# Last group's value product from 32x32 tiles without the DRAM trip, two output tiles ahead of it, last stores on two queues

## The chip, the core and the metric

One core of a Trainium2 chip runs the kernel. The metric is device time in microseconds for one execution; the kernel before takes 1820.34 us (median of 3 runs, 1820.07 to 1821.33). TensorE multiplies, VectorE (DVE) and ScalarE (ACT) work on SBUF and PSUM, GpSimd (POOL) on SBUF, SyncE (SP) mainly issues DMAs.

## What is computed

A cross attention over 32 batches of 512 tokens, 640 channels, 20 heads of 32, with 77 context tokens a batch, then an output projection with bias and the residual. All in fp32. (The reference has three more attention branches; the context has only 77 tokens, so their slices are empty and they add nothing.)

```python
q = _heads(hidden_states @ to_q_w)
h_txt = _sdpa(q, _heads(ehs_txt @ to_k_w), _heads(ehs_txt @ to_v_w))
...
s = jnp.einsum('bhqd,bhkd->bhqk', q, k) * scale      # in _sdpa
p = jax.nn.softmax(s, axis=-1)
return jnp.einsum('bhqk,bhkd->bhqd', p, v)
...
out = _merge(h_txt) + ...
out = out @ to_out_w + to_out_b
out = (out + residual) / RESCALE
```

## The kernel before

It has two stages. `project_context` (about the first 300 us) computes keys and values of all batches and leaves them in DRAM (`k_scratch`, `v_scratch`). `attend` goes over 32 batches, and in each over 5 groups of 4 heads (128 channels). Group n = 5 b + g, 0 to 159. Most matmuls of the projections are three passes over operands split into a high and a low part (`project_q` L750, `project_out` L789: 5 channel chunks x 3 passes = 15 matmuls of 512 columns for one tile).

A group's steps: `scores` (L765, 16 matmuls, each on 32 rows of the array, into four PSUM banks `s_bank`, one for a head), `maxima` (DVE L638), `exps` (ACT L597), `reciprocals` (DVE L644), `normalise` (POOL L574), `turn_probs` (DVE L654: 32x32 squares of the probabilities are transposed into `turned`). The squares are not yet a matrix with the 77 context tokens on the partitions: SyncE writes `turned` to DRAM (`write_probs`, L522, 768 KB) and reads it back in three pieces (`read_probs`, L530) into `probs_t`, which has tokens on 77 partitions and 512 queries along the free dimension. In `turned` partition i*32+s holds context token s of a 32-token block, for the queries of row block i. `sum_values` (L777) multiplies values and probabilities, 4 matmuls, one for a head, each 77 rows by 32 columns by 512 moving. Its result is copied by `ot_high_part` (ACT L604) and the remainder by `ot_low_part` (DVE L665) into `o_t`. `project_out` of tile k (L789) reads `o_t` of all five groups of a batch; `add_output` (DVE L685) adds bias and residual, `turn_output` (DVE L692) turns the tile into `out_blocks`, and `store_out` (SP L518) sends it out in four DMAs once all five tiles are turned. There is one `out_blocks`, so `turn_output` of a batch waits until the stores of the batch before have landed.

The order on each engine is written by hand in strings, one for each group of a batch. In the one of TensorE, S is the scores, Q the query projection of the next group, V the value product of the group two back, O and P an output tile of the batch before or the one before that:

```python
TENSOR = orders("S Q0 Q1 Q2 Q3 Q4 P3 V",
                "S Q0 Q1 Q2 Q3 Q4 P4 V",
                "S Q0 Q1 Q2 Q3 Q4 O0 V",
                "S Q0 Q1 Q2 Q3 Q4 O1 V",
                "S O2 Q0 Q1 Q2 Q3 Q4 V")
```

What the last batch leaves open stands behind the loop: the value products of groups 158 and 159, tiles 3 and 4 of batch 30, and the five tiles of batch 31. `project_out` writes two PSUM banks in turn, so tile n waits until tile n - 2 has been added (`out_added`).

## Time and profile before

| | us |
|---|---|
| median of 3 runs | 1820.34 |
| lowest, highest | 1820.07, 1821.33 |
| the profiled run | 1821.04 |
| its span, first to last instruction | 1819.2 |

The profile is one execution. PE is TensorE's matmuls, PEld its weight loads, which overlap them. Times in its rows count from the start of the span. A row of a timeline merges instructions of one kind: start, time that it covers, engine, line, operation, what it writes and reads, how many (an fp32 matmul leaves two records, so four are x8), and in brackets how long the engine had been idle and what ended that. "SPq" rows are DMA issues on SyncE.

### The profile page before, as it was taken

The page shows a single profiled execution, that of the slowest core. Times are in us where ns is not written, and L with a number is a line of the kernel's source. Part 1 is how long each engine was busy: PE and PEld are TensorE (multiplying, and loading weights), DVE is VectorE, ACT ScalarE, POOL GpSimd, SP SyncE. Part 2 cuts the span into 40 slices and gives each one's busy share as a digit, 9 for nine tenths or more (in the row PEclk, how much of TensorE's full clock was granted, in tenths as well). Part 3 has the DMA queues.
Part 4 walks back from the last instruction along what each step waited for, and adds up shares of the span by engine and source line. Part 5 has one row for each costly group of instructions (what it writes and reads, how often), then busy time and mean ns, then how long its engine had stood idle before and what let it go on. Part 6 is the DMA issues. An engine that isn't in the chain of part 4 may idle for free.

```text
span 1819.2 us, 38127 instructions
## 1 busy us (share of the span) xinstructions
PE 1756.4 (97%) x13360; PEld 1364.8 (75%) x13360; DVE 1282.9 (71%) x2506; ACT 1052.6 (58%) x5597; POOL 496.5 (27%) x735
## 2 busy tenths in 40 slices
PE   7999996799999999999999999999999999999996
PEld 7999995567777777777777777777777777777764
DVE  5321201678888888888888888888888888888873
ACT  4321211666666666666666666666666666666660
POOL 1111110333333333333333333333333333333330
PEclk9999998899999999999999999999999999999998
DMA  9543112587888888888888888888888888888863
GB/s 229 152 121 92 63 47 58 142 204 214 224 220 223 222 222 224 226 219 221 225 227 219 223 223 223 230 215 222 223 224 229 217 224 223 223 224 224 220 185 103
DMA packets 311599, 357.00 MB, mean 196 GB/s; under 512 B 40240, under 2 KB 194592, under 8 KB 311408
## 3 DMA queue, kind: packets, MB, share of 16 engines
q1 hardware_dynamic: 241648, 301.30, 61.0%
q10 hardware_dynamic: 65472, 40.64, 10.4%
q0 software_dynamic: 4288, 12.62, 2.0%
q8 instruction: 106, 1.74, 0.4%
q14 instruction: 85, 0.70, 0.1%
HBM read 174.10 MB, written 180.39 MB: 195 GB/s over the span
## 4 chain that ended last, share of the span: by engine, by line
PE 78%; DVE 2%; ACT 1%; DMA 1%; issue 1%; POOL 0%; SPq 0%; ACTq 0%; DVEq 0%
PE p_bank L750 31%; PE p_bank L789 29%; PE p_scores L765 9%; PE p_bank L777 8%; ACT probs L597 1%; DVE negmax L638 0%; DMA p_scratch<-turned 0%; DMA out<-out_blocks 0%; DVE turned L654 0%; POOL probs L574 0%; DMA probs_t<-p_scratch 0%; DVE x_t L676 0%; DVE x_raw L671 0%; DVE out_blocks L692 0%; SPq L518 0%
## 5 line engine op out<-in xcount | busy, mean ns | idle before, releaser
L597 ACT ACTIVATE probs<-p_scores,negmax 128x77 f32<-128x77 f32 x2560 | 788.7, 361 | 325.9 <-DVE negmax L638 325.9
L574 POOL TENSOR_TENSOR probs<-probs,rsum 128x308 f32<-128x308 f32 x640 | 447.4, 701 | 1021.1 <-DVE rsum L644 1021.0
L597 ACT ACTIVATION_READ_ACCUMULATOR probs<-p_scores,negmax 128x1 f32 x2560 | 619.5, 242 | 0.0
L750 PE MATMUL p_bank<-x_t,wq_split 128*128 128x512 f32 x2400 | 596.4, 401 | 16.0 <-DVE x_t L676 16.0
L789 PE MATMUL p_bank<-o_t,wo_split 128*128 128x512 f32 x2400 | 574.9, 391 | 0.4 <-DVE x_turned L685 0.4
L750 PEld LDWEIGHTS p_bank<-x_t,wq_split 128*128 128x128 f32 x2400 | 446.8, 190 | 116.3 <-DVE x_t L676 17.2
L789 PEld LDWEIGHTS p_bank<-o_t,wo_split 128*128 128x128 f32 x2400 | 448.7, 188 | 98.0 <-issue 2.5
L654 DVE STREAM_TRANSPOSE turned<-probs 128x384 f32<-128x384 f32 x640 | 352.4, 551 | 39.9 <-POOL probs L574 39.8
L765 PEld LDWEIGHTS p_scores<-k_sb,q_t 32*128 32x128 f32 x5120 | 159.8, 187 | 152.8 <-issue 152.8
L638 DVE TENSOR_REDUCE negmax<-p_scores 128x16 f32<-128x1232 f32 x160 | 230.2, 1438 | 24.0 <-PE p_scores L765 23.8
L604 ACT ACTIVATE o_t<-p_bank 128x512 fp32r<-128x512 f32 x160 | 98.5, 616 | 177.3 <-PE p_bank L777 177.3
L765 PE MATMUL p_scores<-k_sb,q_t 32*128 32x77 f32 x5120 | 182.5, 279 | 18.6 <-ACT probs L597 11.6
L644 DVE RECIPROCAL rsum<-sums 128x4 f32<-128x4 f32 x640 | 107.5, 168 | 125.7 <-ACT probs L597 121.2
L777 PE MATMUL p_bank<-probs_t,v_sb 77*32 77x512 f32 x1280 | 171.3, 607 | 8.6 <-DMA probs_t<-p_scratch 6.3
L661 DVE COPY q_t<-p_bank 128x512 f32<-128x512 f32 x160 | 109.4, 684 | 81.4 <-PE p_bank L750 81.4
L377 PE MATMUL p_bank<-ctx_t,wk_split 128*128 128x256 f32 (+1 forms) x1200 | 147.2, 285 | 9.9 <-DVE wk_split L315 9.6
L377 PEld LDWEIGHTS p_bank<-ctx_t,wk_split 128*128 128x128 f32 x1200 | 146.2, 195 | 10.2 <-DVE wk_split L315 9.6
L397 PE MATMUL p_bank<-wv_split,ctx_t 128*128 128x320 f32 (+1 forms) x960 | 142.2, 309 | 0.0
L397 PEld LDWEIGHTS p_bank<-wv_split,ctx_t 128*128 128x128 f32 (+1 forms) x960 | 139.0, 184 | 1.7
L333 DVE TENSOR_TENSOR ctx_t<-ctx_turned,ctx_t 128x512 fp32r<-128x512 f32 (+1 forms) x40 | 26.7, 668 | 149.1 <-ACT ctx_t L264 148.9
L665 DVE TENSOR_TENSOR o_t<-p_bank,o_t 128x512 fp32r<-128x512 f32 x160 | 108.8, 680 | 0.0
L280 ACT ACTIVATE kv_out<-p_bank 128x320 f32<-128x320 f32 (+1 forms) x40 | 17.5, 437 | 113.0 <-PE p_bank L397 108.0
(30 smaller groups left out, 706.7 us busy)
## 6 DMA issues: line engine op xcount, KB each, us to landing
p_scratch<-turned SPq DMA_DIRECT2D x160, 768.0 KB, 5.9
probs_t<-p_scratch SPq DMA_DIRECT2D x320, 256.0 KB
out<-out_blocks SPq DMA_DIRECT2D x128, 320.0 KB, 5.5
x_raw<-in_x ACTq DMA_DIRECT2D x124, 320.0 KB, 4.4
probs_t<-p_scratch SPq DMA_DIRECT2D x160, 104.0 KB
ctx_raw<-in_ctx SPq DMA_DIRECT2D x32, 256.0 KB, 8.6
k_sb<-k_scratch SPq DMA_DIRECT2D x32, 192.5 KB, 5.1
v_sb<-v_scratch SPq DMA_DIRECT2D x160, 38.5 KB
```

The lines of the kernel that those rows point to most:

```text
L377: last = nc.tensor.matmul(bank[n % BANKS][:, 0:tokens], wk_s[:, a, k, m * P:(m + 1) * P], ctx_t[j % 2][:, b, k, 0:tokens], start=k == 0 an ...
L397: last = nc.tensor.matmul(bank[n % BANKS][0:rows, 0:HALF], ctx_t[j % 2][:, a, k, t0:t0 + rows], wv_s[:, b, k, hf * HALF:(hf + 1) * HALF], ...
L574: nc.gpsimd.tensor_tensor(heads_of(t), heads_of(t), rsum[:, slot, t, :].unsqueeze(2).to_broadcast([P, HG, N_TXT]), ALU.mult).then_inc(prob ...
L597: last = nc.scalar.activation(heads_of(t)[:, h, :], s_bank[:, h, t * N_TXT:(t + 1) * N_TXT], ACT.Exp, bias=negmax[:, slot, t, h:h + 1], ac ...
L638: nc.vector.tensor_reduce(negmax[:, slot, :, :], s_bank[:, :, 0:QT * N_TXT].rearrange("p h (t k) -> p t h k", k=N_TXT), AX.X, ALU.max, neg ...
L654: nc.vector.transpose(turned[slot][:, :, :, t, :].rearrange("p k h q -> p h k q"), squares_of(t)).then_inc(probs_turned, 1)
L661: nc.vector.tensor_copy(tiles_of(q_t[slot][:, :]), rows_of(q_bank[:, :])).then_inc(q_ready, 1)
L665: nc.vector.tensor_tensor(o_t[parity][:, 1, g, :], pv_bank[:, :], o_t[parity][:, 0, g, :].bitcast(F32), ALU.subtract).then_inc(ot_ready, 1)
L750: last = nc.tensor.matmul(q_bank[:, :], wq_s[:, w, c, g * P:(g + 1) * P], x_t[:, a, c, :], start=c == 0 and i == 0, stop=c == CC - 1 and i ...
L765: last = nc.tensor.matmul(s_bank[:, h, t * N_TXT:(t + 1) * N_TXT], q_t[slot][rows, t * P:(t + 1) * P], k_sb[parity][rows, g, :], start=Tru ...
L777: last = nc.tensor.matmul(pv_bank[h * HD:(h + 1) * HD, :], v_sb[:, g, h * HD:(h + 1) * HD], probs_t[slot][:, :, h, :], start=True, stop=True)
L789: last = nc.tensor.matmul(fill_bank[n % 2][:, :], wo_s[:, w, c, k * P:(k + 1) * P], o_t[parity][:, o, c, :], start=c == 0 and i == 0, stop ...
```

## The change

The value product of group 159 no longer reads `probs_t`. `turned` is used directly: for each block of 32 context tokens (k, the last with 13), each head h and each row block i, one matmul takes 32 rows of `v_end` (values of the last group, loaded four times, once for each block of 32 partitions) and 128 queries of `turned`, and accumulates over k. The result for row block i goes to bank i of the score banks. That is 48 matmuls. ScalarE's high part and VectorE's low part of that group then read the four score banks. `write_probs` and `read_probs` of group 159 are gone; eight small loads of `v_end` are issued on SyncE at the start of the stage. Tiles 3 and 4 of batch 30 are moved ahead of the value products of groups 158 and 159, and VectorE's steps on them with them. Of the last four stores ScalarE issues two.

```diff
+TENSOR_END = orders("S O2 V O3 O4")
...
+        v_end = sbuf("v_end", [P, KB, P])
...
+        def end_columns(part):
+            return o_t[(B - 1) % 2][:, part, CC - 1, :].rearrange("p (i c) -> p i c", c=P)
...
-                for kind, k in order[g]:
+                for kind, k in (TENSOR_END[0] if order is TENSOR and last and g == CC - 1 else order[g]):
...
+            heads = slice((CC - 1) * P, CC * P)
+            for i in range(P // SQ):
+                t0 = (B - 1) * N_TXT
+                sp.dma_start(v_end[i * SQ:(i + 1) * SQ, 0:KB - 1, :],
+                             v_scratch[t0:t0 + (KB - 1) * SQ, heads].rearrange("(k s) c -> s k c", s=SQ))\
+                  .then_inc(v_end_loaded, DMA)
+                sp.dma_start(v_end[i * SQ:i * SQ + REST, KB - 1, :],
+                             v_scratch[t0 + (KB - 1) * SQ:t0 + N_TXT, heads]).then_inc(v_end_loaded, DMA)
...
-                        if n + 2 < CC * B:
+                        if n + 2 < CC * B - 1:
                             load_v(*divmod(n + 2, CC))
...
-                    write_probs(n, slot)
+                    if n < CC * B - 1:
+                        write_probs(n, slot)
...
-            sp.wait_ge(pv_done, CC * B - 2)
-            read_probs(CC * B - 1, (CC * B - 1) % 2)
-            for b in (B - 2, B - 1):
-                for i in range(P // SQ):
-                    store_out(b, i)
+            for i in range(P // SQ):
+                store_out(B - 2, i)
+            for i in (0, 1):
+                store_out(B - 1, i)
...
-            for g in (CC - 2, CC - 1):
-                ot_high_part(B - 1, g, (B - 1) % 2)
+            ot_high_part(B - 1, CC - 2, (B - 1) % 2)
+            act.wait_ge(pv_done, CC * B)
+            nc.scalar.activation(end_columns(0), s_bank[:, :, 0:P], ACT.Copy).then_inc(ot_high, 1)
+            for i in (2, 3):
+                act.wait_ge(out_turned, CC * B)
+                act.dma_start(out_v[B - 1][i], out_blocks[i * SQ:(i + 1) * SQ, :, :]).then_inc(out_stored, DMA)
...
             add_output(B - 2, 3)
+            add_output(B - 2, 4)
             turn_output(B - 2, 3)
             ot_low_part(B - 1, CC - 2, (B - 1) % 2)
-            add_output(B - 2, 4)
+            dve.wait_ge(ot_high, CC * B)
+            nc.vector.tensor_tensor(end_columns(1), s_bank[:, :, 0:P], end_columns(0).bitcast(F32),
+                                    ALU.subtract).then_inc(ot_ready, 1)
             turn_output(B - 2, 4)
-            ot_low_part(B - 1, CC - 1, (B - 1) % 2)
...
             sum_values(B - 1, CC - 2, (CC * B - 2) % 2)
-            project_out(B - 2, 3, (B - 2) % 2)
-            sum_values(B - 1, CC - 1, (CC * B - 1) % 2)
-            project_out(B - 2, 4, (B - 2) % 2)
+            pe.wait_ge(v_end_loaded, DMA * 2 * (P // SQ))
+            pe.wait_ge(probs_turned, TILES * B)
+            pe.sem_inc(scores_clear, 1)
+            for k in range(KB):
+                for h in range(HG):
+                    for i in range(P // SQ):
+                        rows = slice(i * SQ, i * SQ + (SQ if k < KB - 1 else REST))
+                        last = nc.tensor.matmul(s_bank[h * HD:(h + 1) * HD, i, 0:P],
+                                                v_end[rows, k, h * HD:(h + 1) * HD],
+                                                turned[(CC * B - 1) % 2][rows, k, h, :, :],
+                                                start=k == 0, stop=k == KB - 1)
+            last.then_inc(pv_done, 1)
```

TensorE from the last output tile inside the loop (tile 2 of batch 30) to the first two tiles of batch 31, before. p2_bank1 is the bank of the value products, p2_bank2 and p2_bank3 those of the output tiles; o_t0 belongs to batch 30, o_t1 to batch 31.

```order
L789 MATMUL p2_bank2<-o_t0,wo_split 128x512 x15
L777 MATMUL p2_bank1<-probs_t1,v_sb 32x512 x4
L777 MATMUL p2_bank1<-probs_t0,v_sb 32x512 x4
L789 MATMUL p2_bank3<-o_t0,wo_split 128x512 x15
L777 MATMUL p2_bank1<-probs_t1,v_sb 32x512 x4
L789 MATMUL p2_bank2<-o_t0,wo_split 128x512 x15
L789 MATMUL p2_bank3<-o_t1,wo_split 128x512 x15
```

The same stretch after the change (line numbers are those of the changed kernel, L789 is L810 there, L777 is L798).

```order
L810 MATMUL p2_bank2<-o_t0,wo_split 128x512 x15
L798 MATMUL p2_bank1<-probs_t1,v_sb 32x512 x4
L810 MATMUL p2_bank3<-o_t0,wo_split 128x512 x15
L810 MATMUL p2_bank2<-o_t0,wo_split 128x512 x15
L798 MATMUL p2_bank1<-probs_t0,v_sb 32x512 x4
L840 MATMUL p2_scores<-turned1,v_end 32x128 x48
L810 MATMUL p2_bank3<-o_t1,wo_split 128x512 x15
```

The two output tiles of batch 30 now stand between the products of groups 157 and 158, and the product of group 159 is 48 matmuls into the score banks.

VectorE from the low part of group 157 to the first addition of batch 31, before (x_raw holds the tiles of batch 30, x_turned1 those of batch 31):

```order
L665 TENSOR_TENSOR o_t1<-p2_bank1,o_t1 128x512
L692 STREAM_TRANSPOSE out_blocks<-x_raw 128x16x32 x3
L685 SCALAR_TENSOR_TENSOR x_raw<-p2_bank3,bias_t,x_raw 128x512
L692 STREAM_TRANSPOSE out_blocks<-x_raw 128x16x32
L665 TENSOR_TENSOR o_t1<-p2_bank1,o_t1 128x512
L685 SCALAR_TENSOR_TENSOR x_raw<-p2_bank2,bias_t,x_raw 128x512
L692 STREAM_TRANSPOSE out_blocks<-x_raw 128x16x32
L665 TENSOR_TENSOR o_t1<-p2_bank1,o_t1 128x512
L685 SCALAR_TENSOR_TENSOR x_turned1<-p2_bank3,bias_t,x_turned1 128x512
```

And after:

```order
L684 TENSOR_TENSOR o_t1<-p2_bank1,o_t1 128x512
L711 STREAM_TRANSPOSE out_blocks<-x_raw 128x16x32 x3
L704 SCALAR_TENSOR_TENSOR x_raw<-p2_bank3,bias_t,x_raw 128x512
L704 SCALAR_TENSOR_TENSOR x_raw<-p2_bank2,bias_t,x_raw 128x512
L711 STREAM_TRANSPOSE out_blocks<-x_raw 128x16x32
L684 TENSOR_TENSOR o_t1<-p2_bank1,o_t1 128x512
L753 TENSOR_TENSOR o_t1<-p2_scores,o_t1 128x512
L711 STREAM_TRANSPOSE out_blocks<-x_raw 128x16x32
L704 SCALAR_TENSOR_TENSOR x_turned1<-p2_bank3,bias_t,x_turned1 128x512
```

Tile 4's addition moved ahead of tile 3's turn, and the low part of group 159 ahead of tile 4's turn.

## Rows read from the trace of the kernel before

**Rows 1.** The page: busy time of the engines; TensorE's granted clock in 40 slices.

```profile
PE 1756.4 (97%) x13360; PEld 1364.8 (75%) x13360; DVE 1282.9 (71%) x2506; ACT 1052.6 (58%) x5597; POOL 496.5 (27%) x735
...
PEclk9999998899999999999999999999999999999998
```

**Rows 2.** Timeline of TensorE, last 50 us: start, us, what, idle before.

```profile
1771.58 1.06 PE L777 MATMUL p_bank<-probs_t,v_sb 77*32 77x512 f32 x8
...
1778.43 1.93 PE L777 MATMUL p_bank<-probs_t,v_sb 77*32 77x512 f32 x8 [5.79 <-DMA probs_t<-p_scratch]
...
1787.37 1.07 PE L777 MATMUL p_bank<-probs_t,v_sb 77*32 77x512 f32 x8 [2.21 <-DVE o_t L665]
...
1788.37 13.94 PE L789 MATMUL p_bank<-o_t,wo_split 128*128 128x512 f32 x60
```

**Rows 3.** Chain of waits that ended last, 1770 to 1820: start, us, what.

```profile
1767.14 6.05 DMA p_scratch<-turned
...
1774.09 4.21 DMA probs_t<-p_scratch
...
1792.14 0.76 DVE x_raw L685
...
1792.93 0.72 DVE out_blocks L692
...
1793.67 0.32 SPq L518
...
1795.69 5.52 DMA out<-out_blocks
...
1801.31 0.10 DVE out_blocks L692
...
1802.71 7.15 PE p_bank L789 x30
```

**Rows 4.** Windows: stretch, length, busy of each engine, PEclk, DMA share, GB/s.

```profile
1776.00:1778.00 2.00, 0.00 (x0) 0.00 (x0) 2.00 (x5) 0.00 (x0) 0.00 (x0) 0.50 0.84 224
...
1781.00:1784.00 3.00, 3.00 (x11) 2.39 (x10) 0.00 (x0) 0.02 (x1) 0.00 (x0) 0.71 0.82 199
```

**Rows 5.** Timeline of VectorE and ScalarE around the last value products.

```profile
1776.11 0.65 DVE L665 TENSOR_TENSOR o_t<-p_bank,o_t 128x512 fp32r<-128x512 f32 x1
...
1776.69 1.88 DVE L692 STREAM_TRANSPOSE out_blocks<-x_raw 128x512 f32<-128x512 f32 x3
...
1788.49 0.60 ACT L604 ACTIVATE o_t<-p_bank 128x512 fp32r<-128x512 f32 x1 [7.47 <-PE p_bank L777]
```

**Rows 6.** Windows (busy PE, PEld) of L777, L765; L765's min/median/max ns; L777's loads grouped.

```profile
1771.57:1771.63 0.06, 0.05 (x4) 0.05 (x8) 1.00 1.05 410
1771.63:1772.02 0.39, 0.39 (x4) 0.10 (x8) 1.00 0.69 268
...
1757.81:1758.88 1.07, 1.07 (x32) 0.98 (x32) 1.00 1.12 218
...
L765 PE MATMUL p_scores<-k_sb,q_t x64: 270/270/329, 1757.8 to 1767.8; 32*128 32x77 f32 x64
...
L777 PEld LDWEIGHTS p_bank<-probs_t,v_sb 77*32 77x32 f32 x1280 | 25.3, 108 | 65.6 <-issue 65.6
```

**Rows 7.** The last stores: timeline of SyncE, and windows as in rows 4.

```profile
1811.40 3.59 SPq L518 DMA_DIRECT2D out<-out_blocks  x4
...
1812.50:1813.00 0.50, 0.00 (x0) 0.00 (x0) 0.00 (x0) 0.00 (x0) 0.00 (x0) 1.00 0.90 212
...
1814.00:1815.00 1.00, 0.00 (x0) 0.00 (x0) 0.00 (x0) 0.00 (x0) 0.00 (x0) 0.50 0.92 211
1815.00:1816.00 1.00, 0.00 (x0) 0.00 (x0) 0.00 (x0) 0.00 (x0) 0.00 (x0) 0.50 0.95 234
```

**Rows 8.** SyncE's queue at the start of the attention stage.

```profile
311.27 0.40 SPq L508 DMA_DIRECT2D k_sb<-k_scratch  x1
326.51 0.38 SPq L522 DMA_DIRECT2D p_scratch<-turned  x1
```

More of the change, by code:

```diff
@@ L35 @@
 KB = -(-N_TXT // SQ)
+REST = N_TXT - (KB - 1) * SQ
 ROW = (HG - 1) * N_TXT + KB * SQ + 1
@@ L444, in attend @@
         q_bank, pv_bank, fill_bank = bank[0], bank[1], bank[2:4]
-        bias_loaded = sem("bias_loaded")
+        bias_loaded, v_end_loaded = sem("bias_loaded"), sem("v_end_loaded")
         k_loaded = [sem(f"k_loaded{i}") for i in range(2)]
```

## Prediction

> **What bounds the kernel now.** I read the page first, then the chain of waits over the last 50 us, then TensorE's timeline there, and last the windows for clock and transfers. On the page TensorE is busy for 97% of the span [rows 1], so nearly everywhere a change pays only by what it takes off TensorE. The diff leaves that part alone: up to the score products of the last group (batch 31, group 4; I call it group 159, counting 5 groups a batch from 0) every compute engine runs the same instructions. The last 50 us are different. The reader is to see two holes in TensorE's row: 5.79 us in front of the value product of group 158, which waited for the turned probabilities to come back from DRAM, and 2.21 us in front of that of group 159, which waited for VectorE [rows 2]. The chain says the same: write to DRAM 6.05 us from 1767.14, read back until 1778.30, then output groups of 15 matmuls with VectorE and the stores of batch 30 between them [rows 3]. The stores land at 1801.21, the first turned tile of batch 31 goes into the buffer they leave free, and only then does the second tile of batch 31 get added, which lets TensorE start its fourth group at 1802.71 [rows 3]. The end is thus a ladder, and each rung moved earlier moves the end. In the hole the granted clock also fell: 0.50 over 1776 to 1778 and 0.71 as the mean of 1781 to 1784, that is half clock (1.2 GHz) until about 1782.7 [rows 4]. TensorE had been idle since 1772.6 when it shows.
>
> **Output tiles 3 and 4 of batch 30 move ahead of the value products.** Nothing is added; 30 matmuls fill the hole. The value product of group 157 starts at 1771.58 [rows 2]. From such a product's start to the next instruction it is 0.99 us (1787.37 to 1788.36), and four groups of 15 take 13.94 us, 3.49 each [rows 2]. So tile 3 starts at 1772.57, tile 4 at 1776.06, and group 158's product at 1779.6. Their waits are met: tile 3 needs the addition of tile 1, tile 4 that of tile 2, which VectorE makes in the last group behind its first transposition. Group 158's data are there at 1778.30 [rows 3], 1.3 us early, and its PSUM bank is free, since VectorE has taken the low part of group 157 at 1776.11 to 1776.76 [rows 5]. If its cover were gone (data 1.3 us later) each further microsecond would cost one. The product of group 159 can start 0.99 us later, at **1780.6**, against 1787.37 before. TensorE has then had no hole, so I count it at full clock.
>
> **The DRAM trip of group 159 goes.** A write of 768 KB and three reads leave SyncE's queue. By then they are no longer on the chain (the wait there is for VectorE), so by themselves they are worth nothing; they are what allows the order above. The wait in their place, for the last transposition, is met at 1776.2: the row behind it on VectorE starts at 1776.11 [rows 5].
>
> **The new product: 48 matmuls of 32x32 tiles, 128 columns, in place of 4 with 77 rows, 32 columns and 512 columns moving.** This form is not in the trace. Each fp32 matmul leaves two records, so 96. Near rows: in the old product all eight weight loads and the first four matmul records are in flight within 0.06 us, and these four stay alone until 1772.02 [rows 6]. So four column tiles run at once, and a record of 512 columns holds its tile some 0.43 us, which is 0.108 us for 128 columns. The score products are 32-row tiles, four row groups at once: 32 records in 1.07 us [rows 6]. Lower bound: all 16 tiles at once, 6 records each, 6 x 0.108 = 0.65 us. Upper bound from these rows: the score products' pace, 96 x 1.07/32 = 3.2 us. Between them I take the order as written: 12 sets of four row tiles, the two records of a set behind one another, the next set (other columns of the array) starting as the second record starts. That is 12 x (0.108 + 0.026 for four starts, the eight loads in 0.06 us being the row for it) = **1.6 us**. It is nearer the low end because the old product shows column tiles over the same rows overlapping; the high end comes from a row whose weight loads have 128 columns, and these have 32.
>
> The Trainium skill, "TensorE: Matmul & The Clock Gate", Part 3 (the mechanism), says that weight loads overlap matmuls in flight only when the row groups differ. The old product's rows speak against it, since its eight loads share their rows. What the rule would give here is rival B.
>
> **From the new product to the stores of batch 30.** VectorE now adds tile 4 before it turns tile 3. Tile 4 is ready at 1779.75, so: add 0.76, turn 0.7, then low part of group 158 at about 1781.35 to 1782.0 (the product at 1779.6, its copy on ScalarE 1.12 later as 1788.49 follows 1787.37 [rows 2, 5]). TensorE needs that at 1780.6 + 1.6 = 1782.2, so it hides; with a product under 1.4 us it would be late next. Then 0.1 us to ScalarE, copy out of the score banks 0.60, low part 0.65, the turn of tile 4 with its store issued 0.74 behind its start (1792.93 to 1793.67), 0.1 of gaps [rows 3, 5]: 2.2 us. I price the copy and the subtraction over four banks like those over one, 512 elements each. First store of batch 30: 1780.6 + 1.6 + 2.2 = 1784.4, against 1793.67 [rows 3]: **9.25 us earlier**. In front of that turn stands VectorE's wait for ScalarE; behind it only the turn and the additions of batch 31 queue, the first of which is not ready before 1785.8.
>
> **Who is last then.** Through the stores: the fourth group of batch 31 started at 1802.71 [rows 3], 9.04 us after the first store of batch 30, so at 1793.45. Through TensorE: tile 0 at 1782.25, three groups of 3.49, 1792.7. The stores stay last by 0.7 us and the gain is 9.25. Both move one for one with the new product: gain = 10.85 - its length.
>
> **Last stores from two queues.** Before, four issues take 3.59 us on SyncE, yet the transfer engines are 0.90 busy from 1812.5 at 212 GB/s, and give 234 once issuing has ended at 1815 [rows 7]. The engines are the limit, not the queue. Bounds: nothing, or all 1.31 MB (4 x 320 KB) at 234 instead of about 212: 6.2 - 5.6 = 0.6 us; a loss of 0.3 if two queues interleave badly. I take **0.3**.
>
> **Start of the stage.** Eight small loads more on SyncE behind the five value loads. At the 0.40 us of an issue [rows 8] they hold the queue from 311.3 to about 314.5; behind them stands the load of batch 1's keys, not used before batch 1, and the first write of probabilities at 326.51 [rows 8]. Cost nothing; if the cover of 12 us were gone, 3.2 us.
>
> **Sum.** 9.25 + 0.3 = 9.55 us. The profiled span of 1819.2 becomes 1809.65, its run of 1821.04 becomes 1811.5. That run stands 0.7 above the median of 1820.34, so against the median the forecast is **1810.8 us** (0.5% faster).
>
> **Rivals.**
> A. All 16 tiles run freely, 0.65 to 1.0 us. VectorE's low part of group 158 (1782.0) is then as late as the product; gain 10.1 + 0.3: 1809.9. For it: eight loads and four matmuls of the old product are under way within 0.06 us [rows 6]. Against: the two records of one tile must follow each other, and no row here shows rows and columns tiled at once.
> B. Loads do not overlap matmuls on the same rows: 24 passes over the four row groups, each 0.108 plus the 0.108 of a load of this width [rows 6], 5.2 us. Gain 5.65 + 0.3: 1814.4. It is what the cited rule of the Trainium skill would do.
> C. TensorE's clock falls once more, since the small tiles leave most of the array unused. Priced by the present fall, half clock from 1776 to 1782.7 [rows 4], 6.8 us: 16 matmuls instead of 30, 3.2 us later on TensorE, 0.7 of it hidden by the stores: 1813.3. Against: the score products are tiles too, and the granted clock stays near full through the batches [rows 1].
> D. Slower. The 96 records don't overlap at all: each waits for the one ahead to leave the array, and a record of the score products lasts 0.27 us from start to end [rows 6]. 96 x 0.27 = 26 us, against the 10.85 that are there: 1820.34 + 15 = 1835. It turns slower than 0.2% (3.6 us) from 14.5 us, 0.15 a record. Both kinds of tile overlap in this trace, so little speaks for it.
> E. It doesn't do what it says: something I missed keeps TensorE waiting before the products (group 158's data later than 1779.6 by several microseconds), and the end stays within 3 us of 1820.
>
> **Chances.** Forecast, with products of 1.2 to 3.2 us (1809.5 to 1812.4): 0.52. A 0.24, B 0.08, C 0.08, D 0.03, E 0.05. The range must hold 8 in 10: the forecast's and A's ends with the store's bounds (1809.9 - 0.3 - a microsecond for run to run and the start of the stage: 1808.3) and B and C with little to spare: up to 1814.6. A measurement of this kernel can tell some 0.2% from no change; faster by more than that (below 1816.7) 0.92, within it 0.05, slower 0.03.
>
> **What would show it.** TensorE's timeline: no hole between 1767 and the new product; tile 4 of batch 30 ahead of a product at 1779.6; the new product at 1780.6 with its length; granted clock 1.00 from 1770 to the end of the matmuls. The first store of batch 30 at 1784.4, VectorE's wait for it before the turn at about 1792, a hole of under 1 us ahead of TensorE's fourth last group. The last stores: from the first issue (1811.40 before) to the end of the span 7.8 us before, 7.5 after. I am wrong if the clock falls, if the new product lasts over 3.2 us, or if VectorE's order makes TensorE wait behind it.

## The result and the profile after

| | before | after |
|---|---|---|
| median of 4 runs, us | 1820.45 | 1809.76 |
| lowest, highest | 1820.07, 1821.33 | 1808.71, 1810.12 |
| span of the profiled run | 1819.2 | 1807.7 |
| last scores of group 159 start | 1766.89 | 1766.71 |
| from there to the end of the span | 52.3 | 41.0 |
| start of the last transposition to the end of the span | 8.5 | 6.9 |

The ratio after to before is 0.9933 with a 95% interval from 0.9918 to 0.9948, a gain of 12.2 us (9.5 to 14.9). The forecast was 9.55 us and 1810.8. The median of the runs lies in the range that was given (1808.3 to 1814.6); the time that the ratio gives, 0.9933 x 1820.45 = 1808.25, lies just below its lower edge. So more was gained than forecast. The last two lines of the table are the steady measure for what follows. Executions differ by up to 2.6 us before they reach the changed part: the last scores start between 1764.4 and 1767.0 over the kernels below. The way from there to the last transposition repeats far better: five kernels that are alike up to that point (the changed one, the three that only send its last stores otherwise, and the one with the two inner loops exchanged) need 34.02 to 34.08 us for it. The whole stretch became 11.3 us shorter.

The page of the changed kernel:

```profile
span 1807.7 us, 38306 instructions
...
PE 1754.1 (97%) x13448; PEld 1364.1 (75%) x13448; DVE 1282.8 (71%) x2506; ACT 1052.0 (58%) x5597; POOL 495.4 (27%) x735
...
PEclk9999998899999999999999999999999999999999
```

Its timeline of TensorE, where both holes of [rows 2] are gone (L798 is the old value product, L840 the new one, L810 the output tiles):

```profile
1771.40 1.07 PE L798 MATMUL p_bank<-probs_t,v_sb 77*32 77x512 f32 x8
1772.39 7.10 PE L810 MATMUL p_bank<-o_t,wo_split 128*128 128x512 f32 x30
1779.42 1.06 PE L798 MATMUL p_bank<-probs_t,v_sb 77*32 77x512 f32 x8
1780.42 1.49 PE L840 MATMUL p_scores<-turned,v_end 32*32 32x128 f32 x96
1782.02 10.45 PE L810 MATMUL p_bank<-o_t,wo_split 128*128 128x512 f32 x45
1792.84 7.12 PE L810 MATMUL p_bank<-o_t,wo_split 128*128 128x512 f32 x30 [0.36 <-DVE x_turned L704]
```

The chain of waits from the new product to the tile that had to wait for the stores, in answer to [rows 3]:

```profile
1781.94 0.61 ACT o_t L648
...
1782.57 0.03 DVE o_t L753
...
1783.18 0.71 DVE out_blocks L711
...
1783.91 0.32 SPq L525
...
1785.94 5.41 DMA out<-out_blocks
...
1791.44 0.10 DVE out_blocks L711
```

Windows of the changed kernel (columns as in rows 4). From 1770 to 1800 the granted clock is 1.00, where [rows 4] had 0.50 and 0.71. During the last stores the transfers run at 314 and 334 GB/s, where [rows 7] had 211 to 234, and their share is above 1:

```profile
1770.00:1800.00 30.00, 29.47 (x224) 21.82 (x222) 15.27 (x28) 6.09 (x33) 2.80 (x4) 1.00 0.29 72
...
1803.00:1804.00 1.00, 0.00 (x0) 0.00 (x0) 0.00 (x0) 0.00 (x0) 0.00 (x0) 0.50 1.09 314
1804.00:1805.00 1.00, 0.00 (x0) 0.00 (x0) 0.00 (x0) 0.00 (x0) 0.00 (x0) 0.50 1.12 334
```

### The profile page after: what moved, and what is told of

It is laid out like the page before. It is cut to its first block, busy times and chain, and to the rows that moved or that the text cites. A ratio compares the mean times of both kernels' runs of the same rounds, so it can differ in the third digit from the quotient of the medians.

```text
span 1807.7 us, 38306 instructions
## 1 busy us (share of the span) xinstructions
PE 1754.1 (97%) x13448; PEld 1364.1 (75%) x13448; DVE 1282.8 (71%) x2506; ACT 1052.0 (58%) x5597; POOL 495.4 (27%) x735
## 4 chain that ended last, share of the span: by engine, by line
PE 79%; DVE 1%; ACT 1%; issue 1%; DMA 0%; POOL 0%; SPq 0%; ACTq 0%; DVEq 0%
PE p_bank L771 31%; PE p_bank L810 30%; PE p_scores L786 9%; PE p_bank L798 8%; ACT probs L612 1%; DVE negmax L657 0%; DMA out<-out_blocks 0%; DVE turned L673 0%; POOL probs L589 0%; DVE x_t L695 0%; DVE x_raw L690 0%; SPq L525 0%; DVE out_blocks L711 0%; DVE x_turned L704 0%; PE p_scores L840 0%
## 5 line engine op out<-in xcount | busy, mean ns | idle before, releaser
L612 ACT ACTIVATION_READ_ACCUMULATOR probs<-p_scores,negmax 128x1 f32 x2560 | 627.1, 245 | 0.0
L810 PE MATMUL p_bank<-o_t,wo_split 128*128 128x512 f32 x2400 | 573.7, 391 | 0.5 <-DVE x_turned L704 0.4
L810 PEld LDWEIGHTS p_bank<-o_t,wo_split 128*128 128x128 f32 x2400 | 447.9, 188 | 96.1 <-issue 1.2
L798 PE MATMUL p_bank<-probs_t,v_sb 77*32 77x512 f32 x1272 | 169.4, 605 | 0.5 <-DMA probs_t<-p_scratch 0.5
L684 DVE TENSOR_TENSOR o_t<-p_bank,o_t 128x512 fp32r<-128x512 f32 x159 | 108.4, 682 | 0.3 <-ACT o_t L619 0.3
```

What stands on the lines that cost most here:

```text
L612: last = nc.scalar.activation(heads_of(t)[:, h, :], s_bank[:, h, t * N_TXT:(t + 1) * N_TXT], ACT.Exp, bias=negmax[:, slot, t, h:h + 1], ac ...
L684: nc.vector.tensor_tensor(o_t[parity][:, 1, g, :], pv_bank[:, :], o_t[parity][:, 0, g, :].bitcast(F32), ALU.subtract).then_inc(ot_ready, 1)
L798: last = nc.tensor.matmul(pv_bank[h * HD:(h + 1) * HD, :], v_sb[:, g, h * HD:(h + 1) * HD], probs_t[slot][:, :, h, :], start=True, stop=True)
L810: last = nc.tensor.matmul(fill_bank[n % 2][:, :], wo_s[:, w, c, k * P:(k + 1) * P], o_t[parity][:, o, c, :], start=c == 0 and i == 0, stop ...
```

## The experiments

"Stretch" is the time from the start of the last group's scores to the end of the span, 52.3 us before and 41.0 after the change; "tail" the part of it from the start of the last transposition, 8.5 and 6.9. Both are read from one trace of each kernel, whose span is printed to 0.1 us, so a difference can be off by 0.1. Medians are of each kernel's own runs, of executions that also differ ahead of the changed part, so the stretches decide where they and the medians differ by a microsecond.

### The last stores: one queue or two

The changed kernel with all four last stores on SyncE:

```diff
-            for i in (0, 1):
+            for i in range(P // SQ):
                 store_out(B - 1, i)
...
-            for i in (2, 3):
-                act.wait_ge(out_turned, CC * B)
-                act.dma_start(out_v[B - 1][i], out_blocks[i * SQ:(i + 1) * SQ, :, :]).then_inc(out_stored, DMA)
```

> The changed kernel with all four stores of the last batch issued by SyncE, one queue, as before the change; all else as changed. Two theories for the last stretch, which the changed kernel runs in 6.9 us from the start of the last transposition (1800.78) to the end of the span (1807.7), and the kernel before in 8.5 us (1810.66 to 1819.2). Theory 1, the prediction's: the transfer engines were the limit with one queue (0.90 busy), so a second queue is worth 0.3 us and the rest of the 1.6 us comes from elsewhere in the change: this kernel ends in 7.2 us, about 0.3 us slower than the changed one. Theory 2: one queue cannot fill the engines (212 GB/s against 314 to 347 with two), so the whole 1.6 us is the second queue: 8.5 us, about 1.6 us slower, and the rate falls to about 212 again.

Measured: tail 8.5, stretch 42.5, that is 1.6 us longer than the changed kernel's (median 1810.15, ratio to before 0.9942, 0.992 to 0.9964). SyncE's issues and a window of the transfers (timeline, then windows as in rows 4):

```profile
1799.92 3.59 SPq L525 DMA_DIRECT2D out<-out_blocks  x4
...
1802.00:1803.00 1.00, 0.00 (x0) 0.00 (x0) 0.00 (x0) 0.00 (x0) 0.00 (x0) 0.50 0.92 213
```

Theory 2's numbers hold, and theory 1's (7.2 us) does not. The part alone, in the kernel before:

```diff
-            for b in (B - 2, B - 1):
-                for i in range(P // SQ):
-                    store_out(b, i)
+            for i in range(P // SQ):
+                store_out(B - 2, i)
+            for i in (0, 1):
+                store_out(B - 1, i)
...
+            for i in (2, 3):
+                act.wait_ge(out_turned, CC * B)
+                act.dma_start(out_v[B - 1][i], out_blocks[i * SQ:(i + 1) * SQ, :, :]).then_inc(out_stored, DMA)
```

> The kernel before with one part of the change alone: ScalarE issues two of the last four stores. Theory 1 (the transfer engines are the limit): 0.3 us faster than before, 8.2 us from the start of the last transposition to the end of the span. Theory 2 (the one queue is the limit): 1.6 us faster, 6.9 us for that stretch, over 300 GB/s while both queues run.

Measured: tail 7.0, stretch 50.7, 1.6 us less than before (median 1818.68, ratio 0.9988, 0.9974 to 1.0001: the time alone is not clear of zero; the tail, in one trace of each, is 1.6 us shorter). Timeline of SyncE and a window:

```profile
1811.35 0.85 SPq L518 DMA_DIRECT2D out<-out_blocks  x2
...
1814.00:1815.00 1.00, 0.00 (x0) 0.00 (x0) 0.00 (x0) 0.00 (x0) 0.00 (x0) 0.50 1.11 332
```

### Why two queues are faster: the queue, or the partitions that are read

Each store reads one block of 32 partitions. On one queue the blocks go one behind the other; on two queues two blocks are read at a time. To part the two, both queues got the same blocks:

```diff
-            for i in (0, 1):
-                store_out(B - 1, i)
+            sp.wait_ge(out_turned, CC * B)
+            for i in range(P // SQ):
+                sp.dma_start(out_v[B - 1][i][:, 0:8, :], out_blocks[i * SQ:(i + 1) * SQ, 0:8, :])\
+                  .then_inc(out_stored, DMA)
...
+            for i in range(P // SQ):
+                act.dma_start(out_v[B - 1][i][:, 8:16, :], out_blocks[i * SQ:(i + 1) * SQ, 8:16, :])\
+                   .then_inc(out_stored, DMA)
```

> The changed kernel with the last batch's stores divided between the same two queues in another way: SyncE sends the first 256 tokens of all four partition blocks, ScalarE the last 256, so that at each time both queues read the same 32 partitions, and there are eight DMAs of half the size. One queue took 8.5 us from the start of the last transposition to the end, two queues on different partitions 6.9. Theory Q (what a single queue can hand on was the limit): 6.9 us again, over 300 GB/s. Theory S (32 partitions can be read at 212 GB/s and no more, and two queues on different blocks read 64 at a time): 8.5 us, 212 GB/s.

Measured: tail 8.6, stretch 42.7 (median 1809.83, ratio 0.9939, 0.9922 to 0.9956). Two queues, and the rate of one. A window:

```profile
1802.10:1803.10 1.00, 0.00 (x0) 0.00 (x0) 0.00 (x0) 0.00 (x0) 0.00 (x0) 0.50 0.92 207
```

The number of DMAs had doubled too, which left a rival. The control keeps eight half-sized DMAs and parts the blocks:

```diff
+            for i in (0, 1):
+                for n in (0, 8):
+                    sp.dma_start(out_v[B - 1][i][:, n:n + 8, :], out_blocks[i * SQ:(i + 1) * SQ, n:n + 8, :])\
+                      .then_inc(out_stored, DMA)
...
+            for i in (2, 3):
+                for n in (0, 8):
+                    act.dma_start(out_v[B - 1][i][:, n:n + 8, :], out_blocks[i * SQ:(i + 1) * SQ, n:n + 8, :])\
+                       .then_inc(out_stored, DMA)
```

> As e10_same_rows, eight DMAs of half the size on two queues, but each queue with its own partition blocks: SyncE blocks 0 and 1, ScalarE blocks 2 and 3, as in the changed kernel. Theory S (what counts is how many blocks of 32 partitions are read at a time): 6.9 us from the start of the last transposition to the end of the span and over 300 GB/s, as with four DMAs. Theory N (the eight smaller DMAs were what held e10_same_rows to 212 GB/s): 8.5 us.

Measured: tail 7.2, stretch 41.2 (1808.26 in one run).

```profile
1803.00:1804.00 1.00, 0.00 (x0) 0.00 (x0) 0.00 (x0) 0.00 (x0) 0.00 (x0) 0.50 1.05 311
```

Theory N fails. These two kernels differ only in how the same eight DMAs are dealt to the two queues, and the tail differs by 1.4 us. So theory S holds in this: what counts is whether two blocks are read at a time, and not the number of queues. Its figure does not hold as a limit. About 210 GB/s is the rate of the first two blocks. Once their 0.66 MB have left, the third runs at 251 to 282, from one queue (first line, the kernel before) and from two queues on the same block (second line, the kernel above that sends the same rows from both):

```profile
1815.50:1816.00 0.50, 0.00 (x0) 0.00 (x0) 0.00 (x0) 0.00 (x0) 0.00 (x0) 0.50 1.01 282
...
1804.50:1805.00 0.50, 0.00 (x0) 0.00 (x0) 0.00 (x0) 0.00 (x0) 0.00 (x0) 0.50 1.00 271
```

So 32 partitions can be read at more than 212 GB/s, and why the third block is faster is not shown. Two blocks at a time gave 296 to 347 GB/s in half-microsecond windows of full flow. What in the chip sets the pace of a block is not shown either. The blocks of `out_blocks` also go to different columns of the output, so strictly it is "one block and its columns"; reads and writes were not parted, and no kernel gave the blocks to the queues the other way round. The Trainium skill, "DMA: Bandwidth & Descriptors", section "Rules for kernel authors", advises against two transfers to disjoint partition halves, since they serialize. The case here is a near one, stores out of blocks of 32 partitions, and for it the runs show otherwise: the same 1.31 MB took 1.6 us less as two streams from disjoint blocks.

### The order alone and the product alone

The kernel before with the order of the change; group 159 still goes through DRAM, one queue for the stores:

```diff
+TENSOR_END = orders("S O2 V O3 O4")
...
             sum_values(B - 1, CC - 2, (CC * B - 2) % 2)
-            project_out(B - 2, 3, (B - 2) % 2)
             sum_values(B - 1, CC - 1, (CC * B - 1) % 2)
-            project_out(B - 2, 4, (B - 2) % 2)
...
             add_output(B - 2, 3)
+            add_output(B - 2, 4)
             turn_output(B - 2, 3)
             ot_low_part(B - 1, CC - 2, (B - 1) % 2)
-            add_output(B - 2, 4)
```

> The kernel before with the order of the change alone: tiles 3 and 4 of batch 30 stand ahead of the value products, VectorE's steps follow them, but group 159 still goes through DRAM and the last stores are on one queue. TensorE is free at 1780.4; the reads of group 159 were issued at 1779.9 to 1781 before, and land, at the 5.0 us of the reads ahead of them, about 1784.5. If the gain is the order and the trip through DRAM only the remaining wait: product of group 159 at 1784.6 in place of 1787.37 and its end at 1785.6, that is 3.6 us behind the changed kernel's 1782.0 and a gain of 9.7 - 3.6 = 6.1 us over the kernel before. If the hole of 4 us lets the granted clock fall again as in the kernel before, 3.2 us of that goes on TensorE (0.4 hidden behind the stores): gain 3.3 us. Rival: the order alone gives nearly all of the 9.7 us (reads landing by 1781), and the new product is not what pays.

Measured: stretch 48.0, 4.3 us less than before; median 1816.38, ratio 0.9976 (0.9964 to 0.9988). TensorE's timeline, a window and the chain's read:

```profile
1784.56 1.94 PE L778 MATMUL p_bank<-probs_t,v_sb 77*32 77x512 f32 x8 [4.48 <-DMA probs_t<-p_scratch]
1786.42 18.47 PE L790 MATMUL p_bank<-o_t,wo_split 128*128 128x512 f32 x75
...
1784.00:1786.00 2.00, 1.45 (x8) 0.23 (x8) 0.00 (x0) 0.00 (x0) 0.00 (x0) 0.50 0.92 216
...
1780.06 4.36 DMA probs_t<-p_scratch
```

The data came when expected, and behind the hole of 4.48 us the granted clock was 0.50 (window 1784 to 1786), the second of the cases put on record. The rival, that the order alone gives nearly all of the 9.7 us, is refuted. The price of the clock was less than the 3.2 us taken for it: 0.9 us on the product (1.86 against 0.99 to the next instruction) and 1.2 us on the tiles (75 in 18.47 us, against 17.25 in the kernel with both stores split, below), since much of the half-clock time lay in the hole. Half clock costs only what is run in it.

The other part alone: the changed kernel with the order of the kernel before and one queue. The new product stands between tiles 3 and 4.

```diff
-TENSOR_END = orders("S O2 V O3 O4")
+TENSOR_END = orders("S O2 V")
...
             sum_values(B - 1, CC - 2, (CC * B - 2) % 2)
+            project_out(B - 2, 3, (B - 2) % 2)
             pe.wait_ge(v_end_loaded, DMA * 2 * (P // SQ))
...
             last.then_inc(pv_done, 1)
+            project_out(B - 2, 4, (B - 2) % 2)
```

> The changed kernel with the order of the kernel before and one queue for the last stores: the new product stands between tiles 3 and 4 of batch 30, where the old one stood. It needs no free bank of the value products, so VectorE's 2.21 us wait goes, and it is 0.6 us longer than the old one (1.57 against 0.99). The hole of 5.79 us ahead of group 158 and the half clock behind it stay. Expected: 1.6 us faster than the kernel before. Rival: if the new product were what pays most, and the order little, over 5 us faster.

Measured: stretch 50.0, 2.3 us less than before; median 1818.44, ratio 0.9987 (0.9978 to 0.9997). Expected was 1.6. Of the other 0.7, 0.35 is the product of group 158, whose data landed earlier in this execution (it starts at 1778.08 against 1778.43), and 0.15 a new product that took 1.42 us to the next instruction and not 1.57. Half clock stands behind the hole here too: a mean of 0.71 from 1781 to 1784, as before.

```profile
1778.08 1.93 PE L795 MATMUL p_bank<-probs_t,v_sb 77*32 77x512 f32 x8 [5.47 <-DMA probs_t<-p_scratch]
1779.94 4.98 PE L807 MATMUL p_bank<-o_t,wo_split 128*128 128x512 f32 x15
1784.85 1.49 PE L838 MATMUL p_scores<-turned,v_end 32*32 32x128 f32 x96
1786.27 13.89 PE L807 MATMUL p_bank<-o_t,wo_split 128*128 128x512 f32 x60
```

So the order alone gives 4.3, the product alone 2.3, both together 9.8 (the changed kernel on one queue: 52.3 - 42.5). Some 3 us come only with both. Each alone leaves a hole (4.48 and 5.47 us) and half clock behind it; the changed kernel has neither.

### What the new product's length hangs on

The loops over heads and row blocks exchanged:

```diff
             for k in range(KB):
-                for h in range(HG):
-                    for i in range(P // SQ):
+                for i in range(P // SQ):
+                    for h in range(HG):
```

> The changed kernel with the loops over heads and row blocks of the new product exchanged: four matmuls in a row now share their 32 rows of the array and differ in columns, where in the changed kernel they differ in rows and share the columns. By the rows of the old product (column tiles over the same rows run at once) this costs nothing: 1.5 to 1.7 us. By the rule that weight loads overlap matmuls in flight only on other rows, each of the 96 passes waits for its load: with 0.108 for the load and 0.108 for the columns, up to 96 x 0.216 / 4 = 5.2 us if rows still overlap between fours, and 20 us if they do not.

Measured, timeline of TensorE: the product starts at 1778.48 and the next instruction at 1780.08, 1.60 us, as in the changed kernel; stretch 41.0.

```profile
1778.48 1.49 PE L840 MATMUL p_scores<-turned,v_end 32*32 32x128 f32 x96
1780.08 10.46 PE L810 MATMUL p_bank<-o_t,wo_split 128*128 128x512 f32 x45
```

The next instruction does not show the product's end, though. Tile 0 of batch 31 waits for `ot_ready`, that is for VectorE's low part of group 158, as well, and that is what came last. In the changed kernel, VectorE (L684) and the first weight load of the tile:

```profile
1781.18 0.69 DVE L684 TENSOR_TENSOR o_t<-p_bank,o_t 128x512 fp32r<-128x512 f32 x1 [0.28 <-ACT o_t L619]
...
1781.99 2.12 PEld L810 LDWEIGHTS p_bank<-o_t,wo_split 128*128 128x128 f32 x10 [0.36 <-issue]
```

VectorE ends at 1781.87 and the load starts 0.12 us later; with the loops exchanged it is 1779.94 and 0.11. In the kernel with the product alone, above, this wait does not stand behind the product, and the next instruction starts 1.42 us after it. ScalarE, which waits for the product only, starts 1.52 us after the product's start in the changed kernel, 1.52 with the loops exchanged and 1.53 in that kernel. So the product itself takes 1.42 us in both orders, and the other 0.18 us of the 1.60 is TensorE waiting for VectorE.

The loop over token blocks innermost, so that one 32x32 tile gets its six records in a row:

```diff
-            for k in range(KB):
-                for h in range(HG):
-                    for i in range(P // SQ):
+            for h in range(HG):
+                for i in range(P // SQ):
+                    for k in range(KB):
```

> The changed kernel with the new product's loop over the three token blocks innermost: three matmuls (six records) in a row on the same 32x32 tile of the array. If matmuls start in the order written and a tile is held 0.108 us by a record, the six must follow one another and only the last of a tile overlaps the first of the next: 16 x 5 to 16 x 6 records one behind the other, 8.6 to 10.4 us. If tiles are served freely, whatever the order: 1.6 us as now.

Measured: 4.49 us (1779.95 to 1784.44), stretch 44.1.

```profile
1779.95 4.56 PE L840 MATMUL p_scores<-turned,v_end 32*32 32x128 f32 x96
1784.44 10.49 PE L810 MATMUL p_bank<-o_t,wo_split 128*128 128x512 f32 x45
```

Neither number was right: 8.6 to 10.4 if each record holds back all behind it, 1.6 if tiles are served in any order. The order of tiles matters, but two to three tiles still overlap: 16 tiles in 4.49 us is 0.28 us a tile, where six records at the 0.108 us of the prediction would be 0.65. How the array hands them out is open. What the run does show is the rest of the path: the product is 3.1 us longer than 1.42 and the end comes 3.1 us later, so it moves with the product one for one.

The 48 matmuls twice, and three times:

```diff
+            for k in range(KB):
+                for h in range(HG):
+                    for i in range(P // SQ):
+                        ... (the same matmul again)
```

> The changed kernel with the 48 matmuls of the new product run twice (the second time writes the same result again). The prediction says that the gain falls one for one with the product's length: 3.14 us in place of 1.57, first store of batch 30 1.57 us later, end of the matmuls 1.57 us later. Rival: a start-up cost in the first 1.57 us that the second run doesn't pay, so well under 3.1; or part of it hidden behind the stores' wait, so the end moves less than the product.

> The changed kernel with the 48 matmuls of the new product run three times. Run twice, the product did not take 2 x 1.57 = 3.1 us but 4.3: after 173 of 192 records TensorE stood for 1.36 us, releaser 'issue'. Theory F (instructions come to the engine in loads of 16 KB, and 96 records with their weight loads in 1.2 us use them up faster than they are brought): with three times the gaps recur as the number of instructions grows, two or more gaps of 1 to 2 us, 7 us or more in all. Theory O (one stall of that place, not of the supply): one gap, about 4.7 + 1.4 = 6.1 us in all.

Measured, from the product's start to the next instruction: 4.3 us for two (1778.15 to 1782.47), 5.5 for three (1778.97 to 1784.45), against 1.42 for one. Stretches 44.8 and 45.0. Both have one hole, ahead of the 174th record; the first lines are of two, the last two of three:

```profile
1779.38 1.33 PE L848 MATMUL p_scores<-turned,v_end 32*32 32x128 f32 x74
1782.08 0.47 PE L848 MATMUL p_scores<-turned,v_end 13*32 13x128 f32 x19 [1.36 <-issue]
1782.47 18.91 PE L810 MATMUL p_bank<-o_t,wo_split 128*128 128x512 f32 x75
...
1780.20 1.33 PE L848 MATMUL p_scores<-turned,v_end 32*32 32x128 f32 x74
1782.73 0.36 PE L848 MATMUL p_scores<-turned,v_end 13*32 13x128 f32 x10 [1.19 <-issue]
```

Less the idle time shown, two products come to 3.0 us and three to 4.3, so each costs 1.4 to 1.5 us, as one alone does, and there is no start-up cost to speak of. What theory F forecast (two or more holes, 7 us or more) did not come, and theory O's one hole fits, with 5.5 us in place of 6.1. But the second hole of theory F may lie beyond the 288 records. Two transfers of instructions stand near the hole in the trace of two, one about 1 us ahead of it and one about 1 us behind it. What makes the hole is left open.

With three, the end comes 4.1 us later for a product 4.1 us longer, one for one again. With two it comes 3.8 us later for 2.9. There TensorE's clock was at half for a while (a mean of 0.82 from 1785 to 1790), and the 75 matmuls behind the product took 18.91 us, against 17.94 with the short hole in the changed kernel, which is the rest within 0.1.

### Going on from there

The stores of batch 30 on two queues as well:

```diff
+            for b in (B - 2, B - 1):
+                for i in (0, 1):
+                    store_out(b, i)
...
+            for b in (B - 2, B - 1):
+                for i in (2, 3):
+                    act.wait_ge(out_turned, CC * (b + 1))
+                    act.dma_start(out_v[b][i], out_blocks[i * SQ:(i + 1) * SQ, :, :]).then_inc(out_stored, DMA)
```

> The changed kernel with the stores of batch 30 also on two queues. They land about 1.6 us earlier (theory 2, one queue is the limit), so VectorE's wait of 4.97 us for them shrinks to 3.4; TensorE's hole of 0.36 us ahead of its fourth last group goes, and TensorE is then last: 0.36 us faster than the changed kernel, no more. By theory 1 (transfer engines are the limit) the stores land 0.3 us earlier and 0.3 us is gained.

Measured: stretch 40.3, 0.7 us less than the changed kernel; median 1808.25 (6 runs), ratio 0.993 (0.9916 to 0.9944). The wait for the stores shrinks by 1.6 us and TensorE's hole goes; the wait's line and TensorE's:

```profile
DVE out_blocks L711 <- DMA out<-out_blocks: 3.4, 1, 3.4
...
1782.31 17.25 PE L810 MATMUL p_bank<-o_t,wo_split 128*128 128x512 f32 x75
```

75 matmuls in 17.25 us, where the changed kernel needs 17.94 from 1782.02 to the end of its two pieces. Expected was 0.36 us, the idle time of the hole alone. The matmuls on its two sides took another 0.3 us more than 75 without a hole; that this is the restart of overlapping matmuls is my reading and was not tested.

GpSimd as a third queue, for the fourth store:

```diff
-                for i in (2, 3):
+                for i in ((2, 3) if b < B - 1 else (2,)):
...
+            pool.wait_ge(out_turned, CC * B)
+            pool.dma_start(out_v[B - 1][3], out_blocks[3 * SQ:4 * SQ, :, :]).then_inc(out_pooled, DMA)
```

> The kernel with both batches' stores on two queues (e9_both_split), and in the last batch GpSimd's queue takes the fourth store: SyncE two, ScalarE one, GpSimd one. Theory Q with the engines far from full: up to 1.5 times the rate of two queues, the last landing 1 us or more earlier, 5.9 us from the start of the last transposition to the end. Engines full with two queues (their share stood at 1.1 and 314 to 347 GB/s): 6.9 us, or a little more, since GpSimd's DMAs take longer to start.

Measured: tail 7.4, stretch 40.8, 0.5 us longer than with two (median 1808.94, ratio 0.9936, 0.9916 to 0.9956). Its DMAs (issues, KB each, us to landing): GpSimd's takes longest. It moved its 0.33 MB in 96 packets, where ScalarE's took 528, so the run compares more than the number of queues, and it does not tell whether two queues fill the transfer engines.

```profile
out<-out_blocks SPq DMA_DIRECT2D x2, 320.0 KB, 4.1
out<-out_blocks ACTq DMA_DIRECT2D x1, 320.0 KB, 3.9
out<-out_blocks POOLq DMA_DIRECT2D x1, 320.0 KB, 5.9
```

The last batch's stores in two parts, on the two queues:

```diff
+            for tiles, c0, c1 in ((CC - 1, 0, CQ - SQ), (CC, CQ - SQ, CQ)):
+                for i in (0, 1):
+                    sp.wait_ge(out_turned, CC * (B - 1) + tiles)
+                    sp.dma_start(out_v[B - 1][i][:, :, c0:c1], out_blocks[i * SQ:(i + 1) * SQ, :, c0:c1])\
+                      .then_inc(out_stored, DMA)
```

> The kernel with both batches' stores on two queues (e9_both_split), and the last batch is stored in two parts: the 128 columns of tiles 0 to 3 of each block as soon as tile 3 is turned, the last 32 columns at the end. The end then waits for 0.26 MB in 2048 pieces of 128 bytes in place of 1.31 MB in 2048 pieces of 640. If a piece costs by its number (640 bytes took 38 and 32 ns on an engine): the tail stays at 6.9 us. If by its bytes: 0.26 of 1.31 MB, 0.8 us in place of 4.0 us, a tail of 3.7 us and 3.2 us gained over e9. In between, with 15 to 20 ns for a short piece: 1.5 to 2 us gained.

Measured: tail 4.6, stretch 38.1; median 1805.41 (5 runs), ratio 0.9916 (0.9901 to 0.9931), the fastest of all kernels here. Its DMAs:

```profile
out<-out_blocks SPq DMA_DIRECT2D x2, 256.0 KB, 3.7
out<-out_blocks ACTq DMA_DIRECT2D x2, 256.0 KB, 4.2
out<-out_blocks SPq DMA_DIRECT2D x2, 64.0 KB, 2.6
out<-out_blocks ACTq DMA_DIRECT2D x2, 64.0 KB, 2.9
```

Four fifths of the bytes are sent from the turn of tile 3 on, while the last tile is computed, added and turned. The short pieces ran at 185 to 202 GB/s and still win: 2.2 us off the end, 2.9 us under the changed kernel in all. That lies between the 3.2 us of a cost by bytes and the 1.5 to 2 us of 15 to 20 ns a piece.

## Why the prediction was right and where it missed

**What bounds the end.** Right. The holes closed and the end moved with them.

**Tiles 3 and 4 ahead; the waits.** Right, once the 0.18 us is taken off by which the whole execution ran ahead (last scores at 1766.71 against 1766.89): tile 3 forecast 1772.57, seen 1772.39; product of group 158 1779.6, seen 1779.42; new product 1780.6, seen 1780.42. The match to the hundredth is partly luck of rounding: the terms give 1779.55 and 1780.54, 0.05 and 0.06 us less. The clock stayed at 1.00.

**The DRAM trip.** The prediction said that it is worth nothing by itself and allows the order. Nearly so: the order is possible with the trip and gave 4.3 us, but then the reads of group 159 end last and leave a hole of 4.48 us.

**The new product.** Forecast 1.6 us between bounds of 0.65 and 3.2. TensorE's next instruction came 1.60 us after it (1780.42 to 1782.02), which looks exact and is luck: the product took 1.42, and 0.18 was a wait for VectorE. The picture behind the number is right only in part. I had derived it from sets of four tiles in the order written, and the exchanged loops kept the length. Yet six records of one tile in a row took 4.5 us, not the 8.6 that the same picture gives there. Rival B, which goes by the rule on row groups that the prediction cites, is refuted for this form: with the shared rows innermost the expectation by it was 5.2 us, and ScalarE could start after 1.52.

**From the product to the first store, and who is last.** The prediction had VectorE's low part of group 158 hidden behind the product, and named 1.4 us as the length below which it would be late. It was late, by the 0.18 us above, which is one of the signs of being wrong that the prediction lists. The end does not show it, since TensorE stood 0.36 us for the stores later on. Forecast first store 1784.4, seen 1783.91, 3.49 us from the product's start in place of 3.8: 0.18 is the shorter product and 0.1 the turn, which starts 0.61 us behind the start of the subtraction. Fourth group forecast 1793.45, seen 1792.84. The matmuls' end and the last transposition came 9.9 us earlier, 9.7 without the 0.18 of the execution, against 9.25. The stores stayed last, as said, with 0.36 us of idle time in front of TensorE.

**The last stores. The step that failed.** The prediction said of a share of 0.90 at 212 GB/s: "The engines are the limit, not the queue", bounded the second queue by the 234 GB/s behind the last issue at 0.6 us, and took 0.3. The term measured 1.6 us (tail 8.5 to 6.9), when it was taken out of the changed kernel, and again when it was put alone into the kernel before. The share is a busy time that can pass 1 (1.12 with two queues), so 0.90 was not a full engine. The trace before had signs of it. A window of [rows 6] shows 410 GB/s at a share of 1.05, for other transfers. And the 234 GB/s that bounded the gain is the mean of two unlike halves, 187 and 282 GB/s (1815.0 to 1815.5, and the first of the two lines on the third block above): the same queue and the same stores ran at 282 in the second. At that rate 1.31 MB take 4.7 us and not 5.6, so the bound of 0.6 us was too low as well. With 1.6 in its place the sum would have been 9.25 + 1.6 = 10.85 us, or 1809.5. The measured shortening of the stretch is 11.3 us; the other 0.45 is the 9.7 against 9.25 of the paragraph above: 0.18 the product, 0.1 the turn, and 0.1 the way from the first store to the fourth group (8.93 us in place of 9.04).

**The start of the stage.** Eight loads on SyncE, expected to cost nothing. They hold the queue from 311.77 to 315.18, the load of batch 1's keys follows at 315.22 (311.27 before), and the first write of probabilities starts at 326.49 (326.51 before). The last scores start 0.18 us earlier than before. So no cost shows.

**The chances.** Faster came. The range's lower end allowed for 0.6 us from the stores, the upper bound of the term that failed, and stood 1.0 us too high for it. Its own terms, 1809.9 - 0.3 - 1, give 1808.6 and not the 1808.3 put on record, and for products of 1.2 us the sum gives 1810.4 and not 1809.5.

## What to carry to other kernels

At the end of a kernel, look at what the last transfers wait for: try giving stores that read different partition blocks to different queues, and send what is ready before the last tile, even if the rest goes in short pieces. A transfer share of 0.9 is no proof that the engines are full; ask what a second stream from other partitions would do. The start of the next instruction gives the length of the one ahead of it only if nothing else held it back: look at what else it waits for (here 0.18 us of the 1.60 were VectorE's). A hole in TensorE can cost more than its length (here the half clock behind holes of 4.5 to 5.8 us), so parts that close it only together are worth more than their sum.

## What the runs showed of the hardware

- Stores from one block of 32 partitions (320 KB in pieces of 640 bytes) ran at 187 to 214 GB/s in the first two blocks, whether one queue issued them or two (kernel before, changed kernel on one queue, same rows from both queues), and at 251 to 282 GB/s in the third; from two blocks at once at 296 to 347 GB/s (changed kernel, its stores alone in the kernel before, halves of different blocks), all in half-microsecond windows of full flow. The tail with all four stores was 8.5 to 8.6 us one block at a time and 6.9 to 7.2 us two at a time.
- The busy share of the transfer engines passes 1: up to 1.13 with two queues and pieces of 640 bytes, 1.30 and 1.37 with pieces of 128 bytes.
- 32x32 tiles in fp32: 48 matmuls (96 records) of 128 columns in 1.42 us to the next instruction, and ScalarE's start behind them within 0.01 us whichever of rows and columns changed fastest; with the same tile six records in a row 4.5 us.
- One idle stretch of 1.2 to 1.4 us with no cause but "issue" after 173 such records, in two kernels at the same place; one pass of 96 records has none.
- Pieces of 128 bytes: 64 KB a DMA landed in 2.6 to 2.9 us, 256 KB in pieces of 512 bytes in 3.7 to 4.2.
